# Cross attention and stream mixing on one core: where the next batch's key logits, the deferred FFN work, the Sinkhorn steps and the last mix matrices stand in each engine's queue

## The reference

```python
# attention, per batch; q = layernorm(x), k = v = context
qh = softmax(Wq q, over the 64 values of a head) * 64**-0.5
kh = softmax(Wk k, over the 2048 positions);  vh = Wv v
context = einsum('hdn,hen->hde', kh, vh)
out = Wo (context^T qh) + bo
x = x + out / norm(out, over channels) * g * 16
# FFN, each of the 4096 rows (batch, channel) is a token of 4 streams of 512
z = layernorm(x); zn = z * rsqrt(mean(z*z) + eps)
res, pre, post = zn @ W_res.T + b, zn @ W_pre.T + b, zn @ W_post.T + b   # 16, 4, 4
H_res = (1-g) I + g * sinkhorn(res, 50 iterations); H_pre, H_post = softmax(pre), softmax(post)
x_pre = sum_n H_pre[n] * stream_n;  y = x_pre @ W_branch
x = x + H_res @ streams + H_post * y
```

## Time and profile before

| | us |
|---|---|
| median of 3 runs (2836.42 to 2837.56) | 2837.36 |
| the profiled execution | 2838.41 |
| its span, first to last instruction | 2836.7 |
| PE busy (share of the span) | 2528.3 (89%) |
| DVE busy | 1715.8 (60%) |
| ACT busy | 1103.8 (39%) |
| POOL busy | 921.2 (32%) |
| mean granted clock of TensorE | 0.961 of 2.4 GHz |

### The profile page before, as it was taken

How to read it: one execution, slowest core, us unless ns; L and a number is a source line. 1 busy time by engine, 2 the same in 40 slices (tenths; PEclk the granted TensorE clock), 3 DMA queues, 4 the chain that set the end, 5 groups by cost and what they waited for, 6 DMA issues and landing times.

```text
span 2836.7 us, 34124 instructions
## 1 busy us (share of the span) xinstructions
PE 2528.3 (89%) x11492; PEld 1838.4 (65%) x11492; DVE 1715.8 (60%) x4226; ACT 1103.8 (39%) x2374; POOL 921.2 (32%) x870
## 2 busy tenths in 40 slices
PE   6989899999989899998989989898998989989853
PEld 5777777777666677666667666666766667666510
DVE  2444534446766757455674867634687685876685
ACT  2434334434333333434334343343433334343322
POOL 2433415060513315061340605224062250521412
PEclk9999999999999999999999999999999999999976
DMA  6112121212112121423323222232323414231254
GB/s 214 45 64 93 60 90 45 94 40 97 52 56 93 60 82 38 136 78 108 123 75 120 84 91 69 84 125 68 126 78 106 124 49 139 77 107 36 80 164 136
DMA packets 200140, 255.65 MB, mean 90 GB/s; under 512 B 43550, under 2 KB 109854, under 8 KB 199966
## 3 DMA queue, kind: packets, MB, share of 16 engines
q1 hardware_dynamic: 199966, 253.47, 28.4%
HBM read 177.53 MB, written 75.89 MB: 89 GB/s over the span
## 4 chain that ended last, share of the span: by engine, by line
PE 72%; DVE 17%; ACT 3%; issue 3%; POOL 2%; DMA 1%; SPq 0%; DVEq 0%; POOLq 0%; ACTq 0%
PE big L666 15%; PE kc_bank L609 15%; PE big L641 13%; PE tb L651 4%; PE tb L708 4%; PE tb L595 3%; PE big L583 3%; PE big L585 3%; PE big L584 3%; PE tb L719 3%; PE misc L688 3%; DVE stats L838 2%; ACT turned L1199 2%; PE kc_bank L685 1%; DVE ska L1015 1%
## 5 line engine op out<-in xcount | busy, mean ns | idle before, releaser
L1199 ACT COPY turned<-tb 128x512 f32<-128x512 f32 x512 | 297.6, 586 | 937.0 <-PE tb L651 660.0
L666 PE MATMUL big<-merged,turned 128*128 128x256 f32 x2048 | 492.9, 383 | 62.4 <-ACT turned L1199 61.0
L609 PE MATMUL kc_bank<-ctxt,turned 128*128 128x256 f32 x2048 | 492.2, 385 | 32.5 <-ACT turned L1199 32.5
L666 PEld LDWEIGHTS big<-merged,turned 128*128 128x128 f32 x2048 | 380.9, 190 | 207.8 <-issue 124.8
L641 PE MATMUL big<-wq,x_sb 128*128 128x512 f32 x1024 | 486.5, 600 | 5.9 <-DVE q_sb L908 5.1
L609 PEld LDWEIGHTS kc_bank<-ctxt,turned 128*128 128x128 f32 x2048 | 379.0, 194 | 89.4 <-issue 46.4
L1414 POOL TENSOR_TENSOR ctx_l<-stage,ctx_h 128x512 fp32r<-128x512 f32 x128 | 164.1, 1283 | 602.5 <-ACT ctx_h L1234 602.5
L1444 POOL TENSOR_TENSOR q_sb<-q_sb,qsum 128x1024 f32<-128x1024 f32 x128 | 243.4, 1901 | 272.8 <-DVE qsum L920 272.8
L811 DVE TENSOR_REDUCE kmax<-big 128x1 f32<-128x512 f32 x256 | 174.6, 686 | 225.9 <-PE big L585 224.9
L719 PE MATMUL tb<-mix_ld,mix_w 121*96 121x512 f32 (+2 forms) x324 | 192.0, 692 | 105.1 <-POOL mix_w L1426 85.6
L641 PEld LDWEIGHTS big<-wq,x_sb 128*128 128x128 f32 x1024 | 181.5, 192 | 157.4 <-issue 146.8
(11 more groups left out here) (137 smaller groups left out, 3692.8 us busy)
## 6 DMA issues: line engine op xcount, KB each, us to landing
mix_ld<-streams SPq DMA_DIRECT2D x157, 240.0 KB
stage<-in_ctx SPq DMA_DIRECT2D x64, 512.0 KB, 5.8
ctxt<-in_ctx_t SPq DMA_DIRECT2D x64, 512.0 KB, 6.4
x_sb<-in_x SPq DMA_DIRECT2D x64, 512.0 KB, 6.3
x_tr<-in_x_t SPq DMA_DIRECT2D x64, 512.0 KB, 6.7
streams<-x_sb SPq DMA_DIRECT2D x64, 512.0 KB, 2.8
out<-mix_out SPq DMA_DIRECT2D x157, 192.0 KB, 2.2
streams<-y_sb SPq DMA_DIRECT2D x32, 256.0 KB, 2.0
```

The source lines that it names most:

```text
L609: t = nc.tensor.matmul(kc_bank[:, 0:C], turned[n % 3][:, j * P:(j + 1) * P], ctxt[:, nt, :], start=nt == 0, stop=nt == NT - 1)
L666: t = nc.tensor.matmul(big[2 + p % 2][:, half], turned[n % 3][:, dt * P:(dt + 1) * P], merged[:, dt, :], start=dt == 0, stop=dt == DT - 1)
L1199: nc.scalar.copy(turned[k % 3][:], tb[n % 2][:]).then_inc(s_tba, 1)
```

## The change

1. PE's drain: from place 16 `return_pair` stands ahead of `attention_out`; the next batch's four key logits stand at places 17, 19, 21, 23 (16, 17, 21, 23 before) and ahead of `attention_out`. DVE's `key_max` follows at 18, 20, 22, 24.
2. `pre` moves from B of round 0 and A of round 1 to B of round 1; `y` of the first half from A and B of round 1 and A of round 2 to the end of round 1 and B of round 2, of the second half from rounds 2 and 3 to the end of B of round 3. The load of the next `x` moves four places down.
3. A Sinkhorn step stands only in `B` of rounds 1 to 3 and in `Q` from place 5 on: 12 + 22 places per batch where it was 16 + 27. Groups 0 and 1 get 116 places in place of 132, so their coefficients come later (place 7 of the queries of batches 7 and 11). With that the mixes shift: eight fewer in batch 7, eight more in batch 10, eight fewer in batch 11, eight more in the tail.
4. Tail: the eleven last matrices are built by DVE between its `own_pair`s (0, 4, 3, 4 of them), and the mixes stand in the same portions.
5. Start: the first batch's context goes into `x_sb[1]`, without a wait; DVE makes `wk_l` and four `ctx_l` of 1024 columns.

```diff
@@ def xattn_ffn, the table of places
-            put(keys[25], "load", b + 1)
+            put(keys[29], "load", b + 1)
...
-            put(keys[7], "pre", b - 1, 0)
-            put(keys[8], "pre", b - 1, 1)
-            put(keys[9], "pre", b - 1, 2)
+            put(keys[12], "pre", b - 1, 0)
+            put(keys[13], "pre", b - 1, 1)
+            put(keys[14], "pre", b - 1, 2)
             for ct in range(CT):
                 for ph in range(6):
-                    put(keys[((10, 12, 13, 14, 15, 16), (18, 20, 21, 22, 23, 24))[ct][ph]], "y", b - 1, ct, ph)
+                    put(keys[((15, 16, 20, 21, 22, 23), (22, 24, 28, 29, 30, 31))[ct][ph]], "y", b - 1, ct, ph)
...
-        free = [place for place in order_of_places[starts[gr]:starts[gr + 1] - 8] if place[0] != "A"]
-        free = free[:SINK * 8 // 7]
+        free = [place for place in order_of_places[starts[gr]:starts[gr + 1] - 8]
+                if place[0] == "B" and place[2] or place[0] == "Q" and place[2] >= 5]
+        free = free[:SINK]
...
     for n in range(CT * STREAMS // 2):
+        put(TAIL, "own first", n)
+    last_made = 0
+    for n, upto in enumerate((0, 4, 7, len(MIX_TILES[LAST]))):
         put(TAIL, "own", n)
-    for n in range(len(MIX_TILES[LAST])):
-        put_mix(TAIL)
-        if n % 3 == 2:
-            put(TAIL, "own store", n // 3)
-    for n in range(len(MIX_TILES[LAST]) // 3, CT * STREAMS // 2):
+        for k in range(last_made, upto):
+            put(TAIL, "last matrix", known - len(MIX_TILES[LAST]) + k)
         put(TAIL, "own store", n)
+        for _ in range(last_made, upto):
+            put(TAIL, "mix", mixed)
+            mixed += 1
+            put_loads(TAIL)
+        last_made = upto
@@ def sync_program
             def load_ctx(b, i):
-                n = b * NQ + i
+                n = (b - 1) * NQ + i
                 if n >= 2:
                     w.wait_ge(s_cl, (n - 1) * CT)
-                elif n:
+                elif n == 1:
                     w.wait_ge(s_wkl, 1)
-                nc.sync.dma_start(stage[i % 2][:],
+                nc.sync.dma_start(staged(b, i),
...
@@ def tensor_program
+                    if b + 1 < NB and i in (17, 19, 21, 23):
+                        key_logits(b + 1, 0, (17, 19, 21, 23).index(i))
+                    if i >= NT and i % 2 == 0 and i < NT + 10:
+                        return_pair(b, (i - 10) // 2)
                     if 5 <= i < NT + 5:
                         attention_out(b, i - 5)
-                    if i >= 10 and i % 2 == 0 and i < NT + 10:
+                    if 10 <= i < NT and i % 2 == 0:
                         return_pair(b, (i - 10) // 2)
-                    if b + 1 < NB and i in (16, 17, 21, 23):
-                        key_logits(b + 1, 0, (16, 17, 21, 23).index(i))
@@ def vector_program
+            w.wait_ge(s_wkh, 1)
+            nc.vector.tensor_tensor(wk_l[:], stage[1][:], f32(wk_h[:]), ALU.subtract).then_inc(s_wkl, 1)
+            for i in range(NQ):
+                w.wait_ge(s_ch, i + 1)
+                nc.vector.tensor_tensor(ctx_l[:, :, quarter(i)], staged(0, i), f32(ctx_h[:, :, quarter(i)]),
+                                        ALU.subtract).then_inc(s_cl0, 1)
...
+            def last_matrix(n):
+                k = n % LOADS
+                w.wait_ge(s_mixld[k], (n // LOADS + 1) * 48)
+                w.wait_ge(s_const, CONSTS)
+                nc.vector.tensor_tensor(mix_w[k][0:ONES, :, :], mix_mask[0:ONES, :].unsqueeze(2).broadcast_to([ONES, TOK, STREAMS]),
+                                        mix_co[k][0:ONES, :].unsqueeze(1).broadcast_to([ONES, TOK, STREAMS]),
+                                        ALU.mult).then_inc(s_lastblk, 1)
```

More of the change, by code:

```diff
@@ L250, in xattn_ffn @@
         s_first = sem("s_first")
+        s_lastblk = sem("s_lastblk")
         s_added = sem("s_added")
@@ L257, in xattn_ffn @@
         s_cl = sem("s_cl")
+        s_cl0 = sem("s_cl0")
         s_wkh = sem("s_wkh")
@@ L372, in xattn_ffn, with staged @@
         maps = [misc[:, ct * MAPS:(ct + 1) * MAPS] for ct in range(CT)]
+        def staged(b, i):
+            return stage[i % 2][:] if b else x_sb[1][:, :, i * BANK:(i + 1) * BANK]
         def f32(ap):
@@ L380, in xattn_ffn @@
         own_tile = (GROUPS[-1] - 1) * CT
+        last_group = len(mix_tiles) - len(MIX_TILES[LAST])
         def kl_count(b, dt, i):
@@ L447, in load_x @@
                     w.wait_ge(s_x[i], b * 16)
+                if b == 1:
+                    w.wait_ge(s_cl0, NQ)
                 if b >= 2:
@@ L575, in key_logits @@
                     w.wait_ge(s_wkl, 1)
-                    w.wait_ge(s_cl, (b * NQ + i + 1) * CT)
+                    if b:
+                        w.wait_ge(s_cl, ((b - 1) * NQ + i + 1) * CT)
+                    else:
+                        w.wait_ge(s_cl0, i + 1)
                     if b and i < 2:
@@ L716, in behind @@
                         w.wait_ge(s_mixld[k], (n // LOADS + 1) * 48)
-                        w.wait_ge(s_blk, n + 1)
+                        if n < last_group:
+                            w.wait_ge(s_blk, n + 1)
+                        else:
+                            w.wait_ge(s_lastblk, n - last_group + 1)
                         weights = mix_w[k][0:ONES + 1, 0:count, :].rearrange("p c i -> p (c i)")
@@ L1128, in behind @@
                         own_pair(task[1])
+                    elif task[0] == "last matrix":
+                        last_matrix(task[1])
                     elif task[0] == "pre":
@@ L1171, in vector_program @@
                         second_stats(b, (i - 14) // 4)
-                    if b + 1 < NB and i in (17, 18, 22, 24):
-                        key_max(b + 1, 0, (17, 18, 22, 24).index(i))
+                    if b + 1 < NB and i in (18, 20, 22, 24):
+                        key_max(b + 1, 0, (18, 20, 22, 24).index(i))
                     if b + 1 < NB and i == 24:
@@ L1233, in context_high @@
                     w.wait_ge(s_kl, kl_count(b - 1, DT - 1, i))
-                nc.scalar.copy(ctx_h[:, :, quarter(i)], stage[i % 2][:]).then_inc(s_ch, 1)
+                nc.scalar.copy(ctx_h[:, :, quarter(i)], staged(b, i)).then_inc(s_ch, 1)
             def start_pre(b, ct):
@@ L1336, in behind @@
                         mix_bank(task[1])
-                    elif task[0] == "own":
+                    elif task[0] == "own first":
                         for k in range(2 * task[1], 2 * task[1] + 2):
@@ L1414, in context_low @@
                 nc.gpsimd.tensor_tensor(ctx_l[:, ct, quarter(i)], stage[i % 2][:, ct, :], f32(ctx_h[:, ct, quarter(i)]), ALU.subtract).then_inc(s_cl, 1)
-            w.wait_ge(s_wkh, 1)
-            nc.gpsimd.tensor_tensor(wk_l[:], stage[1][:], f32(wk_h[:]), ALU.subtract).then_inc(s_wkl, 1)
-            for i in range(NQ):
-                for ct in range(CT):
-                    context_low(0, i, ct)
             def mix_matrix(n):
```

## The result

The changed kernel takes 2741.68 us in the median of 4 runs (2739.90 to 2743.04), the one before 2836.89 beside it: ratio 0.9667 (95% interval 0.9655 to 0.9679), 95 us less. The forecast was 2720 in 2690 to 2772. Its profiled execution has a span of 2738.2 us.

The account below looks back on a forecast made before the run. PE, busy 89% of the span, was taken as the bound, its 308 us idle being many small waits; 10.6 + 33 + 38 + 28 - 12 + 13 + 7 = 117.6 us off 2838.41 gave a median of 2720, range 2690 to 2772.

Parts of the forecast that it names:

- Start: Kernel start: five context loads go out at once, key logits start at 22.7 instead of 33.3; gain 10.6 us.
- Drain: End of each batch: `attention_out` no longer waits for `turned`; gain 2.8, 1.9 or 1.2 us a batch, 33 in all.
- Batch starts and mixes: First rounds of batches: `key_context` waits less for its copies, gain 38 us; eight fewer mixes in the loop, gain 7.
- mix term: Mixes out of the loop: eight fewer stand on PE's path, about 0.9 us each; gain 7 us (4 to 10).
- Places 0 to 4: First five query places without Sinkhorn steps: 2.8 us each in 10 batches, gain 28 us, at most 36.
- Density: Query places 5 to 14: more Sinkhorn steps per place on DVE; loss 12 us, bounds 3 and 35.
- Tail: After the loop: DVE builds all eleven last matrices, so POOL's no longer stand until DVE is through; gain 13 us.
- (a): Rival: DVE becomes the bound of every batch with steps; only 69 us gained, so 2768 us; chance 0.14.
- (b): Rival: the chain's links lose the cover of `y`'s products; slower than before, 2847 us at 1.4 per link; chance 0.03.
- (d): Rival: waits are only renamed, `return_pair` waiting for `add_pair` and links taking over; 45 us gained, so 2793; chance 0.06.

Follow-up runs that it names:

- b_drain: The kernel before with part 1 alone (the drain's order on PE and its key maxima on DVE): 2805.2 us, ratio 0.9900.
- b_sink: The kernel before with part 3 alone (places of the Sinkhorn steps): 2803.4 us, ratio 0.9888.
- a_rp3_late12: The changed kernel with `return_pair` of pair 3 behind `attention_out` of tile 11 again in batches 12 to 15 alone: 2731.3 us, ratio 0.9626 to the kernel before.
- a_add_first: The changed kernel with POOL's `add_pair` of pair 3 ahead of `query_normalise` of pair 6 at place 15: 2731.6 us, ratio 0.9632 to the kernel before.

## Why the prediction was right, and where it was not

The sum was 117.6 us; the spans differ by 98.5, the medians by 95.2. The time lies in the range, but that the sum came so near is partly luck. Two terms fell short (drain by 20.9, batch starts with the mixes by 24.8) and two were better than forecast (places 0 to 4 by 14.1, density by 12.4).

- **Start**: forecast 10.6. The first key logits stand at 21.39, before at 33.39: 12.0, since `wmap` lands at 14.57 and not near 16. 0.9 of it is lost again in the first round.
- **Drain**: forecast 33, measured 12.1. In batches 0 to 11 it gave 38.2, more than the 28.2 there (3.8 a plain batch, forecast 2.8). The step that failed is "1.2 in batches 12 to 15": I allowed for a `return_pair` that comes 1.83 us earlier by shrinking the gain and not by its own price. These drains lost 26.1 us: 9.2 by the order alone, 15.0 by the density alone (b_drain, b_sink), with a granted clock of 0.90 to 0.97 in them where it was 0.99 to 1.00. And 11.6 of the 26.1 are in batch 15 alone, whose drain has no key logits to stand between; the forecast took it for one like the others.
- **Batch starts and mixes**: forecast 38 and 7, measured 38.8 in the rounds and -18.6 in the last places before them, 20 together. The 38 came as worked out: 9.7 in batches 1 to 3 (forecast 9), 1.5 in batch 0, where the granted clock is 1.00 and was 0.96, 32.0 in 4 to 7 and 11 (forecast 25), 1.5 in batch 10, and -6.0 in the others. What failed beside it is the mix term, forecast as a gain of 7. Of the 18.6 lost, 7.3 are at the end of batch 9 (1.9 before, 9.2 after), where the mixes that moved to batch 10 now wait 6.4 us for POOL's matrix; the forecast saw that wait come and took 2 off for it. 5.9 are behind batches 12 to 14, where the wait was there before and grew. Part 3 alone loses 13.0 at these places (b_sink) and part 1 alone 5.9 (b_drain); what the moved mixes and what the denser steps cost in part 3 wasn't tried apart.
- **Places 0 to 4**: forecast 28 of at most 36 in 10 batches; measured 42.1, since they give 2.2 in batches 7 and 11 too and up to 5.4 in 12 to 15.
- **Density**: forecast -12, all in places 5 to 14. These cost nothing on balance (-0.4); the price falls later, in the drain and behind it. In b_sink's last four batches it is 15.0 in the drains, 4.7 behind them, 2.8 in places 5 to 14 and 6.2 in the rounds, 28.7 together: inside the bounds (3 to 35), but more than twice the 12. So the drain and the density have to be read together: forecast 21, measured 12.5.
- **Tail**: forecast 13, measured 12.6; the end 38.0 us behind the steps, as said. Inside it two errors cancel: the last matrix came at 2730.57, 4 us later than worked out, as DVE waited for SP's loads five times, and the way from it to the end was 7.6 us and not 11.3.

Of the rivals, (a) had the right place, and in part the mechanism, in batches 12 to 15 alone: there 23 us were lost, of which a_rp3_late12 gives 13.1 back and a_add_first 6.0 by the order of a queue alone, with the same work on DVE. In batches 4 to 11 1.0 steps per place cost nothing in places 5 to 14. (b) didn't show: the chain's links wait 14.4 + 5.2 us now (L637, L642), 5.7 + 9.0 + 11.1 before. What (d) said of `add_pair` is true in four batches, at pair 3, and in batch 15 at pair 4 too.

## What to carry to other kernels

When an instruction moves up in an in-order queue, look at the producer's queue too. Here DVE's result was ready, but the POOL instruction that used it stood behind one that waited for something else. A schedule whose density differs by stage (1.0 steps a place in eight batches, 1.9 in four) needs a rule for each: undoing two edits in a quarter of the batches gave 20 us on top of the 95. The last round of a loop is a case of its own: it lacked the work that hid the wait in the others. And the worth of one part may hang on the others, so test it with and without them.
